# Expert heads of a fused four-layer kernel: the order of projection, scores and products in a round

## The reference

```python
ss = sigmoid(x @ Ws).reshape(b, t, H, E);  sd = sigmoid(x @ Wd).reshape(b, t, H, E)
ms = topk_mask(ss, 3);  md = topk_mask(sd, 3)
ss_g = ss * ms;  sd_g = sd * md
q = einsum('bthed,bthe->bhtd', q5, sd_g)      # q5 = x @ Wq, all 5 experts
k = einsum('bthed,bthe->bhtd', k5, ss_g)      # k5, v5 = x @ Wkv
v = einsum('bthed,bthe->bhtd', v5, ss_g)
attn = softmax(einsum('bhid,bhjd->bhij', q * scale, k), axis=-1)
out = einsum('bhij,bhjd->bihd', attn, v)
o5 = einsum('bthd,dm->bthm', out, Wo).reshape(b, t, H, E, DIM)
return einsum('bthem,bthe->btm', o5, md)
```

## Time and profile before

| | |
|---|---|
| median of 3 executions | 1872.41 us (1870.97 to 1880.14) |
| profiled execution, its own time | 1878.52 us |
| its span, first to last instruction | 1876.6 us |
| mean granted TensorE clock | 0.965 of full |
| TensorE (PE) busy | 1695.8 us, 90% of the span |
| ScalarE (ACT) busy | 1216.8 us, 65% |
| VectorE (DVE) busy | 1186.0 us, 63% |
| GpSimd (POOL) busy | 892.4 us, 48% |
| odd and even exponentials, line 1078 | x256, 1020 ns each |
| additions of the exponentials, line 936 | x192 of 128x1024 f32, 2410 ns each |
| shares, line 1047 | x1080 recorded, 269.0 us |

### The profile page before, as it was taken

How to read it: one execution, slowest core, us unless ns; L and a number is a source line. 1 busy time by engine, 2 the same in 40 slices (tenths; PEclk the granted TensorE clock), 3 DMA queues, 4 the chain that set the end, 5 groups by cost and what they waited for, 6 DMA issues and landing times. The chain is left out here.

```text
span 1876.6 us, 26422 instructions
## 1 busy us (share of the span) xinstructions
PE 1695.8 (90%) x9454; PEld 867.2 (46%) x9454; DVE 1186.0 (63%) x1900; ACT 1216.8 (65%) x2359; POOL 892.4 (48%) x542
## 2 busy tenths in 40 slices
PE   7888569999999999999999999779999999898975
PEld 3434256555565555655555555324333333332354
DVE  6887987997779887698877667531414223120296
ACT  2122104766767476766677576668999999999833
POOL 3555305788776678756787677850000000000033
PEclk9999789999999999999999999979999999999988
DMA  3000032212112111211121110130221312201001
GB/s 86 0 11 1 1 117 81 86 44 86 54 44 60 39 54 44 65 40 54 38 65 54 44 54 23 57 124 23 68 91 42 116 45 69 83 31 37 1 12 36
DMA packets 38379, 97.65 MB, mean 52 GB/s; under 512 B 5008, under 2 KB 15968, under 8 KB 38112
## 3 DMA queue, kind: packets, MB, share of 16 engines
q1 hardware_dynamic: 38240, 95.86, 16.4%
HBM read 50.23 MB, written 28.84 MB: 42 GB/s over the span
## 5 line engine op out<-in xcount | busy, mean ns | idle before, releaser
L936 POOL TENSOR_TENSOR b_psum<-b_psum,b_probs 128x1024 f32<-128x1024 f32 x192 | 462.8, 2410 | 221.3 <-ACT b_probs L1078 215.0
L2369 ACT ACTIVATE c_probs<-banks 128x1024 f32<-128x1024 f32 x512 | 483.6, 1029 | 38.5 <-PE banks L2418 23.0
L1078 ACT ACTIVATE b_probs<-banks 128x1024 f32<-128x1024 f32 x256 | 255.4, 1020 | 230.0 <-PE banks L1218 229.3
L1183 PE MATMUL banks<-b_w,b_xh 128*128 128x480 f32 x1024 | 355.1, 399 | 34.2 <-issue 14.2
L1428 DVE TENSOR_TENSOR b_gated<-banks,b_g 128x480 f32<-128x480 f32 x512 | 310.2, 652 | 111.8 <-PE banks L1183 101.4
L1444 DVE TENSOR_REDUCE b_tok<-b_gated 128x192 f32<-128x960 f32 x256 | 281.3, 1137 | 0.5
L1047 ACT ACTIVATE b_share<-b_o,b_picked 128x64 f32<-128x64 f32 x1080 | 269.0, 340 | 1.7 <-DVE b_o L1469 1.7
L2432 PE MATMUL banks<-c_probs,c_vg 128*32 128x512 f32 x2048 | 251.0, 608 | 3.0 <-DVEq L2483 2.7
L1253 PE MATMUL banks<-b_probs,b_tok 128*64 128x512 f32 x1024 | 251.1, 611 | 2.6 <-ACT b_probs L1078 2.6
L1183 PEld LDWEIGHTS banks<-b_w,b_xh 128*128 128x128 f32 x1024 | 194.9, 190 | 117.8 <-issue 59.8
L1218 PE MATMUL banks<-b_qq,b_kk 64*128 64x512 f32 x1536 | 231.3, 424 | 5.4 <-DVE b_gated L1428 4.6
(11 more groups left out here) (248 smaller groups left out, 1807.6 us busy)
## 6 DMA issues: line engine op xcount, KB each, us to landing
b_w<-b_split_w SPq DMA_DIRECT2D x24, 960.0 KB, 4.7
b_kk<-b_kk SPq DMA_DIRECT2D x64, 256.0 KB, 3.6
c_heads<-c_split SPq DMA_DIRECT2D x24, 512.0 KB
c_keys<-c_heads SPq DMA_DIRECT2D x16, 512.0 KB, 3.7
c_queries<-c_heads SPq DMA_DIRECT2D x16, 512.0 KB, 4.7
b_split_w<-b_w SPq DMA_DIRECT2D x8, 960.0 KB, 6.1
b_raw_w<-in_L_ffn_W SPq DMA_DIRECT2D x8, 480.0 KB, 4.1
c_heads<-c_split SPq DMA_DIRECT2D x8, 384.0 KB
```

Of the source, the lines that this page charges most:

```text
L936: nc.gpsimd.tensor_tensor(psum[:, par, :], prev, probs[:, i % 4, :], ALU.add).then_inc(psum_rdy, 1)
L1078: nc.scalar.activation(probs[:, i % 4, :], score_b[i % 2], ACT.Exp).then_inc(exp_rdy, 1)
L1183: last = nc.tensor.matmul(proj_b[u % WAYS][:, 0:HALF_W], a[:, x_of % 2, t * P:(t + 1) * P], w[:, par, part, j, :], start=(i == 0), stop=(i ...
L2369: nc.scalar.activation(probs[:, step % 4, c, :, :], unit_b[u % NU], ACT.Exp, scale=float(HD) ** -0.5).then_inc(exp_rdy, 1)
```

## The change

In a round TensorE now does projection, products, scores instead of projection, scores, products, and of the two score units of a round the odd one comes first. ScalarE takes the exponentials in that order too. The counts that others wait for follow: products and GpSimd's additions name the place of their unit in the new order (`turn_of`), and GpSimd waits for both units of a round; the odd projection tile waits for one exponential fewer.

```diff
+        def turn_of(i):
+
+            return i ^ 1
+
             def add_probs(n, par, i):
-                pool.wait_ge(exp_rdy, EXP0 + NT * n + i + 1)
+                pool.wait_ge(exp_rdy, EXP0 + NT * n + 2 * (i // 2) + 2)
...
             def probabilities(n, i):
-                act.wait_ge(score_ps, NT * n + i + 1)
+                act.wait_ge(score_ps, NT * n + turn_of(i) + 1)
...
-                    for i in (2 * p, 2 * p + 1):
+                    for i in (2 * p + 1, 2 * p):
                         probabilities(n, i)
-                        if p >= 2 and i % 2:
+                        if p >= 2 and i % 2 == 0:
                             copy_slot(slots, f"{p}B")
                         if p >= 2 and not start:
-                            gated_share(n - 1, *before, (2 * i - 8, 2 * i - 7))
+                            at = 2 * turn_of(i) - 8
+                            gated_share(n - 1, *before, (at, at + 1))
...
                     if u % WAYS >= 2 and n >= 2:
 
-                        pe.wait_ge(exp_rdy, EXP0 + NT * (n - 2) + t - 1)
+                        pe.wait_ge(exp_rdy, EXP0 + NT * (n - 2) + t - 2)
...
             def scores(n, par, i, has_next):
-                if i == 0:
+                if i == 1:
                     pe.wait_ge(q_low, n + 1)
                     pe.wait_ge(swapped[par], 32 * (n // 2 + 1))
-                if i % 2 or i == 0 and with_max:
+                if i % 2:
 
                     pe.wait_ge(mult, MULT0 + min(U * (n + 2) + 4 * (i // 2 + 1), U * B * NH))
...
-                pe.wait_ge(exp_rdy, EXP0 + NT * n + i - 1)
+                pe.wait_ge(exp_rdy, EXP0 + NT * n + turn_of(i) - 1)
...
             def products(n, par, i):
-                pe.wait_ge(exp_rdy, EXP0 + NT * n + i + 1)
+                pe.wait_ge(exp_rdy, EXP0 + NT * n + turn_of(i) + 1)
...
-                    for i in steps:
-                        scores(n, par, i, has_next)
                     if p or not start:
                         for i in steps:
                             products(*((n, par, i - 2) if p else (n - 1, 1 - par, NT - 2 + i)))
+                    for i in (2 * p + 1, 2 * p):
+                        scores(n, par, i, has_next)
                     if p == 0 and not start:
                         sum_probs(n - 1, 1 - par)
```

## The result

| | before | after |
|---|---|---|
| median, all executions shown | 1872.39 us (1870.97 to 1880.14, 4) | 1941.51 us (1939.97 to 1942.47, 4) |
| profiled execution | 1878.52 us | 1940.61 us |
| its span | 1876.6 us | 1938.8 us |
| mean granted clock | 0.965 | 0.963 |

The kernel is slower: ratio 1.0359, interval 1.0336 to 1.0383. The forecast was 1914, the range ended at 1940, and the time lies 1.5 us above it. What follows is read from the profiled executions, so the amount to explain is 62 us, against a forecast sum of 41.7.

What follows compares the result with a forecast made beforehand. TensorE's chain in the expert heads was taken as the bound. The terms 15.2 + 3.0 + 29.1 - 9.2 - 1.0 + 4.6 = +41.7 us, added to the 1872.4 us median, gave 1914 us, range 1886 to 1940.

Steps and rivals of the forecast that it cites:

- What bounds the kernel: Expert heads: TensorE is busy 918 of 957 us, so time added to or taken from its chain moves the end.
- Part 1: Rounds 2 to 3: products wait for the late exponential; 7.33 us without slots, 8.36 with four; +15.2 us in all.
- Part 2: Rounds 3 to 0: same loop, 7.33 us without slots, 8.36 where `turn_keys` waits for the last copy; +3.0 us.
- Part 3: Rounds 0 to 1: the sum of probabilities waits about 1.45 us for GpSimd's paired additions in 19 heads; +29.1 us.
- Part 4: Rounds 1 to 2: products cover the odd scores' wait for gates, -9.2 us; VectorE's low part absorbs another -1.
- Part 5: End of the expert heads: two additions instead of one, +2.57 us, and +2 in the last two heads; +4.6 us.
- The changes of tile shape: New neighbours among TensorE's matmul kinds: taken as 0 difference, bounded at -8 and +14 us.
- B: Rival: TensorE reaches the sum after GpSimd's pair is done, part 3 gives nothing; +12.6 us, about 1885; chance 0.16.
- C: Rival: faster, bank 6/7 handed back early is all that counts; 1834 us at full effect, 1853 at half; chance 0.08.
- D: Rival: new waits lower TensorE's clock, 2 us a fall, +40 us in 20 heads, so 1954; chance 0.07.

Runs made afterwards that it cites:

- Both exponentials first: Changed kernel, but ScalarE in rounds 2 and 3 takes both exponentials and slot B's copy before its twenty shares: 1893.82 us, ratio 1.0099.
- The last version: Against the version before it: scores before products where nothing is projected, VectorE sums one tile ahead of the keys (two in gate-preparing heads): 1863.06 us, ratio 0.9939.
- the version before it: Changed kernel with weights earlier, single additions, products in the exponentials' order, and ScalarE's copies and VectorE's sums reordered: 1867.85 us, ratio 0.9944.
- The single line in the old order: Kernel before, with only GpSimd's additions made to wait for both exponentials of their round: 1894.08 us, ratio 1.0094.
- the kernel with the products first: Kernel before, with only its products moved ahead of the scores, even unit first and all counts as before: 2030.72 us, ratio 1.083.

## Why the prediction was right in kind and 27 us short

**What bounds the kernel**: right. TensorE was busy for as long as before (916 us against 918), and the 62 us are time in which it stood or ran at half clock. (That the account adds up proves nothing by itself, since it is made of distances between TensorE's own rows.)

**Part 1, rounds 2 to 3**: right. Forecast 7.33 and 8.36, measured 7.24 and 8.29, with the products waiting 0.90 by the record for the late exponential. The prediction had 1.17 as the time lost; 7.24 - 6.23 = 1.01 was. The three half-slotted heads gained 0.5 each instead of losing 0.09. Both exponentials first took the wait away and left 6.27.

**Part 2, rounds 3 to 0**: right where it looked (7.25 against 7.33, slotted 8.32 against 8.36). It took one loop for all heads without slots and did not ask whether some carry other work on other engines.

**Part 3, GpSimd's pair**: the mechanism and its size are right, 1.5 us in each of 16 heads against 1.45 in 19, with the ends of the sum where they were read (pair done at about +3.0). This is the step that failed all the same, in what it left out. It listed what stands behind the sum in TensorE's queue and not what stands behind the additions in GpSimd's own. The weight job is there, in heads 0 to 4, and in heads 1 to 4 it cost 19.0 us. Head 1 shows how: 12.01 is 1.59 + 3.73 to the first matmul of the projection + 2.70 + 0.53 + 1.87, and 1.59 more, the half clock's part. Putting the job earlier gave exactly these rounds back. Adding singly shortened them to about 8.

A second omission in the same step is smaller. With the sum earlier in the round, its copy on ScalarE is late. The prediction said that this copy would "fit before the next use". It does not: 0.62 a head, seen in the heads that don't wait long at the sum (8.04 to 8.09 instead of 7.45), and in 29 heads once the additions are made singly. In the changed kernel the longer wait hides it in 16 heads. Of the 14 others, seven show it (1, 2, 4, 5, 10, 18 and 26, 4.3 us of the 11.6). Heads 9, 17 and 27 lost the same 0.6 each with 0.4 of wait at the sum. Heads 11 and 19 lost 3.9 there, and their next rounds returned 4.5 (part 4), head 0 has its 1.8 from the cut, and head 3 gained 0.3.

**Part 4, the gates**: right in kind, -12.3 for -9.2; three heads with long waits there (11, 19 and 3) gained 5.7 between them, more than the wait rows showed. In heads 11 and 19, whose wait for VectorE's low part was to absorb the one at the sum, rounds 0 to 2 together changed by -0.9 and +0.3, so it did.

**Part 5, the end**: too small. From round 3 of head 29 to the rotary layer's first scores it takes 81.6 instead of 72.1, +9.5 for +4.6 (11.4 with the 1.87 of the cut). The estimate of 2 for the rounds without projection was the weak term. Head 29 to 30 alone is +4.3, since with nothing projected TensorE follows the exponentials directly. Some 1.6 of it is the clock: behind the wait the products take 3.16 instead of 1.94 and the scores 2.06 instead of 1.66.

```profile
1234.48 3.16 PE L1258 MATMUL banks<-b_probs,b_tok 128*64 128x512 f32 x8 [3.13 <-ACT b_probs L1082]
```

The last version, with the old order there, took 3.0 less from round 3 of head 29 to round 1 of head 30 than the version before it.

**The changes of tile shape**, bounded at -8 and +14: nothing to be seen. Scores 1.59 and products 1.87 have the same distances in the new order (514.84 to 516.71). In head 7's round 1 the four halves, up to what follows them, are 2.78 (518.72 to 521.50, products) and were 2.79 (496.56 to 499.35, scores).

**The rivals.** B, the pair hidden, is refuted: 23 waits, 29.0 us. The single line in the old order shows where it would have held. C, faster, did not come, for the reason given (the exponentials 3.3 apart); brought together, they made these rounds 0.7 shorter than before's. D, the clock: not at the sum, where TensorE idles for 1.43 and stays at full clock, as the shorter of the earlier trace rows let expect. It did come in the four heads with the long stall, 1.6 us in each, 6.3 in the four, and once more behind the wait of 3.13 at the end, places which D did not name. D had put 2 us on a fall.

**Medians.** Of the 27.4 us between 1914 and 1941.5, 20.4 are in the account above. The other 7.0 come from comparing a profiled execution 6.1 above its median with one 0.9 below it. The prediction subtracted this and expected the changed kernel to lie above its median as well; it did not.

## What to carry to other kernels

When a wait is made stricter or a step is moved, write down for each engine everything that is queued behind the waiting instruction, in every variant of the loop body, not in the ordinary one alone: the one job that a few iterations carry extra was more than a quarter of this loss. A consumer moved ahead meets the producer's whole queue. Here products, sum and copies each wanted their own reordering on ScalarE and GpSimd, and the waits covered each other, so that removing one returned less than its price (10 of 19 us, 29 us for the pair only together with the order). Before swapping work on the engine that bounds, place the late half of its producer first: the two exponentials side by side were worth 48 us of the 69. (What that is worth in the kernel before was not tried.)

## What the runs showed of the hardware

- Idle time of 1.43 us at the sum left the clock at full speed in all 16 heads. 2.19 us in the kernel with products in the exponentials' order was followed by a clock of 0.51 and cost some 1.5 us more, but waits of 2.18, 1.97 and 2.14 in heads 7, 12 and 13 were not. 3.65 us behind the weight job was followed by 0.50.
- The length of the gap does not settle it alone. In the kernel with the products first, gaps of 2.29 and 2.30 us before the same instructions were followed by products of 1.94 and of 3.56 us, and in the second case the projection in between still ran at full speed (0.46 for the first matmul). In head 28 of the kernel with products in the exponentials' order a wait of 1.97 was followed by the low clock, the same as in head 12, where it was not; with both exponentials first, four waits of 2.27 to 2.53 in front of the projection were not. The Trainium skill (TensorE: Matmul & The Clock Gate, "Why this matters for your kernels") warns that an idle gap between bursts of matmuls puts the engine back to its low clock, and it warns of gaps longer than all of these. The traces agree on the effect and not on the length: here gaps of 1.97 to 2.31 us were already enough in some heads. A wait 0.7 us longer (2.19 for 1.43) turned a loss of 1.5 us a head into one of 3.8.
- The order in which the three kinds of matmul follow each other cost nothing measurable: the distances were 1.59 over the scores and 1.87 over the products in both orders, and over the four halves of the projection 2.79 with scores behind them and 2.78 with products.
